# Gated delta rule with a ternary MLP: the value blocks are turned by VectorE and a trip through DRAM, not by TensorE

## The reference, cut to what matters

```python
# B=8 sequences, S=512 tokens, H=256; 16 key heads, 32 value heads (R=2 per key head), D=128, chunks of C=128
qkvz  = hidden @ W_qkvz                       # per key head: q, k, two v, two z
mixed = silu(causal_conv4(q | k | v))         # four taps along the sequence, per channel
beta, g = sigmoid(b), -exp(A_log) * softplus(a + dt_bias)
# per head, over chunks i:
T      = inverse(I + tril((beta*k) k^T * decay, -1))
v_new  = T (beta*v) ;  k_cum = T (beta*k*exp(g))
vn     = v_new_i - k_cum_i state
out_i  = (q_i*exp(g)) state + tril(q_i k_i^T * decay) vn
state  = state * exp(g_last) + (k_i*exp(g_last-g))^T vn
x = rmsnorm(out * silu(z)) @ W_out ; then layernorm, a gated MLP with ternary weights, layernorm
```

## Time and profile before

| | before |
|---|---|
| time, median of 3 runs | 4413.36 us (4413.11 to 4414.43) |
| the profiled execution: time | 4417.5 us |
| its span in the trace | 4415.7 us |
| mean granted TensorE clock | 0.989 of full speed |
| busy: PE, DVE, ACT, POOL | 4211.2 us (95%), 3725.5 us (84%), 3842.3 us (87%), 2334.8 us (53%) |
| DMA | 584.82 MB, mean 132 GB/s; 40.6% of 16 engines' time on SP's queue |

### The profile page before, as it was taken

How to read it: one execution, slowest core, us unless ns; L and a number is a source line. 1 busy time by engine, 2 the same in 40 slices (tenths; PEclk the granted TensorE clock), 3 DMA queues, 4 the chain that set the end, 5 groups by cost and what they waited for, 6 DMA issues and landing times. The chain is left out here.

```text
span 4415.7 us, 140088 instructions
## 1 busy us (share of the span) xinstructions
PE 4211.2 (95%) x44246; PEld 3699.2 (84%) x44246; DVE 3725.5 (84%) x6642; ACT 3842.3 (87%) x10855; POOL 2334.8 (53%) x3319
## 2 busy tenths in 40 slices
PE   3799999999999999999999999999999999999788
PEld 2688888888888888888888888888888888888645
DVE  5688888888888888888888888888888888888656
ACT  2699999999999999999999999999999999999655
POOL 3355555555555555555555555555555555555444
PEclk9899999999999999999999999999999999999989
DMA  5544444444444443434343434343434444444200
GB/s 183 179 134 143 134 140 134 140 135 140 137 138 142 132 147 128 151 125 153 123 154 121 154 120 154 120 154 121 153 124 150 129 145 133 141 134 141 70 10 29
DMA packets 450786, 584.82 MB, mean 132 GB/s; under 512 B 237472, under 2 KB 315552, under 8 KB 433184
## 3 DMA queue, kind: packets, MB, share of 16 engines
q1 hardware_dynamic: 449568, 575.59, 40.6%
q10 hardware_dynamic: 1152, 8.39, 0.5%
HBM read 533.81 MB, written 50.07 MB: 132 GB/s over the span
## 5 line engine op out<-in xcount | busy, mean ns | idle before, releaser
L1014 DVE SCALAR_TENSOR_TENSOR conv<-ps,cws,conv 128x511 f32<-128x511 f32 (+2 forms) x1536 | 1084.8, 741 | 59.3 <-ACT conv L892 39.3
L698 PE MATMUL ps<-xb,wb 128*128 128x512 f32 x3072 | 841.8, 409 | 26.0 <-DMA wb<-w_scratch 21.7
L698 PEld LDWEIGHTS ps<-xb,wb 128*128 128x128 f32 x3072 | 541.2, 189 | 129.2 <-issue 30.2
L1057 DVE CAST_PREDICATED pl<-masks,ps 128x512 f16<-128x512 uint16 x768 | 546.8, 712 | 55.3 <-PE ps L760 32.6
L953 ACT ACTIVATE t<-ps 128x512 f16<-128x512 f32 x768 | 465.8, 607 | 118.4 <-PE ps L768 107.3
L1263 POOL TENSOR_TENSOR xo<-xo,zs 128x512 f32<-128x512 f32 x128 | 164.0, 1281 | 714.3 <-DVE xo L1108 714.3
L1263 POOL TENSOR_TENSOR xo<-xo,home 128x512 f32<-128x512 f32 x128 | 163.0, 1273 | 699.8 <-DVE xo L1108 699.8
L957 ACT ACTIVATE u<-ps 128x512 f16<-128x512 f32 x768 | 473.1, 616 | 43.6 <-PE ps L773 43.6
L858 PE MATMUL ps<-wo,xt 128*128 128x256 f32 x3072 | 429.4, 289 | 33.4 <-DVE xt L1114 32.6
L712 PE MATMUL ps<-wb,xb 128*128 128x256 f32 x3072 | 428.3, 289 | 0.0
L858 PEld LDWEIGHTS ps<-wo,xt 128*128 128x128 f32 x3072 | 384.6, 191 | 47.4 <-issue 41.9
(11 more groups left out here) (188 smaller groups left out, 11691.8 us busy)
## 6 DMA issues: line engine op xcount, KB each, us to landing
xb<-x_scratch SPq DMA_DIRECT2D x128, 1024.0 KB, 5.8
wb<-w_scratch SPq DMA_DIRECT2D x128, 1024.0 KB, 5.7
decays<-rows_scratch SPq DMA_DIRECT2D x128, 512.0 KB, 3.7
wb<-w_scratch SPq DMA_DIRECT2D x128, 512.0 KB, 4.3
wo<-wout_scratch SPq DMA_DIRECT2D x128, 512.0 KB, 6.3
rk<-rk_scratch SPq DMA_DIRECT2D x128, 256.0 KB, 4.1
w_scratch<-wsplit SPq DMA_DIRECT2D x128, 192.0 KB, 3.2
wpiece<-in_Wqkvz SPq DMA_DIRECT2D x128, 96.0 KB, 2.5
```

The costliest lines, as they stand in the source:

```text
L698: last = nc.tensor.matmul(proj_bank[c][:, :], wb[:, pw, k * WCOL + c * D:k * WCOL + (c + 1) * D], xb[p][:, px, k * S:(k + 1) * S], start=( ...
L1014: nc.vector.scalar_tensor_tensor(out=conv[c][:, back:S], in0=proj_bank[c][:, 0:S - back], scalar=cws[p][:, c * TAPS + 3 - back:c * TAPS + ...
L1057: nc.vector.copy_predicated(halves(pl[l], l, 0), mask[:, None, :, :].broadcast_to([128, NU, C // (4 << l), 2 << l]), packed(p_bank, l)).th ...
```

## The change

PE no longer turns V0 and V1, and ACT no longer copies them. In their place:

- `flip` (twice, DVE): a transpose of `conv[V0 + h]` in blocks of 32 by 32, 128x512 float32 each time. Inside each group of 32 partitions a block is turned; blocks do not change their group. The output goes to `flip`, which lies in the memory of `et`.
- `move_v` (SP): when both flips are done, four stores, one for each 32-channel part `q`, each of 128 partitions by 1 KB, to `v_dram`, whose rows are ordered so that the DRAM side of each store runs over 4 outer rows, 32 rows inside, and 1 KB each. SP then waits until all four have landed, and loads the whole 512 KB into `vt[p]` with 4 KB for each partition.
- `vt[p]` has a new order, so `residual` reads runs of 32 elements. `residual 0` waits for the load (`vt_in`). `decay` waits for it as well, because `flip` lies in `et`; `flip` waits until `attn` has read `et`.
- `move_v` stands in the list right behind `flip 1`, ahead of `store_split` and `load_raw`.
- In the last iteration the load of the MLP's down weights (`ff_load 0`) moves from the end of one pass to a place behind `move_v` in the next, and waits for `vt_in`.
- Waits of PE, ACT and DVE that guarded the PSUM banks of the two turns go away.

```diff
+    v_dram = nc.dram_tensor("v_scratch", (4, 32, 4, R * NC * 32), f32, kind="Internal").ap()
...
-        vt = [home[:, 1, :].rearrange("p (n h d) -> p n h d", n=NC, h=R), sb("vt1", [128, NC, R, D])]
+        vt = [home[:, 1, :].rearrange("p (w x) -> p w x", w=4), sb("vt1", [128, 4, R * NC * 32])]
...
+        flip = et[:, :, :].rearrange("p (q u) c -> p q (u c)", q=4)
...
+        def values(p):
+            return vt[p][:, :, :].rearrange("p w (h n c) -> p n h w c", h=R, n=NC)
...
-            + at(-1, ("qs_mm", 1)) + at(0, ("turn", V0)) + at(-1, ("residual", 1), ("ff_tern", 0), ("ff_total", 2)) + at(1, ("tap", Q))
-            + at(-1, ("y", 1)) + at(0, ("t_copy", 0), ("small", 0), ("ff_load", 1), ("vt", 0), ("u_mm", 0)) + at(1, ("conv", Q, 1))
...
-               ("u_mm", 1), ("turn", V1), ("low", g0), ("p", 2)) + at(-1, ("ks_mm", 2)) + at(1, ("silu", K)) + at(-1, ("out", 1))
-            + at(0, ("u_copy", 1), ("t_mm", 2), ("vt", 1), ("ff_load", 2)) + at(1, ("split", 0), ("store_split", 0)) + at(2, ("load_raw", 0))
+            + at(-1, ("qs_mm", 1), ("residual", 1), ("ff_tern", 0), ("ff_total", 2)) + at(1, ("tap", Q)) + at(-1, ("y", 1)) + at(0, ("t_copy", 0),
+               ("small", 0), ("ff_load", 1), ("flip", 0), ("u_mm", 0)) + at(1, ("conv", Q, 1)) + at(-1, ("y_copy", 1)) + at(0, ("p_mm", 1))
...
+            + at(-1, ("ks_mm", 2)) + at(1, ("silu", K)) + at(-1, ("out", 1)) + at(0, ("u_copy", 1), ("t_mm", 2), ("flip", 1), ("move_v", 0),
+               ("ff_load", 2), ("ff_load", 0)) + at(1, ("split", 0), ("store_split", 0)) + at(2, ("load_raw", 0)) + at(0, ("u_mm", 2))
...
+            def move_v(a, p, _):
+                sp.wait_ge(flipped.sem, flipped.at(a, 2))
+                res_ready.wait(sp, a - 2, NC)
+                vt_in.wait(sp, a - 1, 16)
+                for q in range(4):
+                    sp.dma_start(v_dram[q].rearrange("r w x -> w r x"), flip[:, q, :]).then_inc(v_out.sem, 16)
+                sp.wait_ge(v_out.sem, v_out.at(a, 64))
+                sp.dma_start(vt[p][:, :, :], v_dram.rearrange("q r w x -> (q r) w x")).then_inc(vt_in.sem, 16)
...
                 if q == 0:
                     sys_ready.wait(sp, a, 2)
                     attn_ready.wait(sp, a, 2)
+                    vt_in.wait(sp, a, 16)
...
-                if c == V0:
-                    xt_low.wait(pe, a - 2, 2) or attn_ready.wait(pe, a, 2)
-                if c == V1:
-                    tapped.wait(pe, a + 1, convolved(K)) or z_ready.wait(pe, a, 1)
...
-            def values(a, p, h):
-                act.wait_ge(turn_mm.sem, turn_mm.at(a, h + 3))
-                res_ready.wait(act, a - 2, NC)
-                nc.scalar.activation(vt[p][:, :, h, :], four(turn_bank[V0 + h]), ACT.Copy).then_inc(vt_ready.sem, 1)
-
             def decay(a, p, g):
...
+                vt_in.wait(act, a - 1, 16)
...
+            def flip_v(a, p, h):
+                ve.wait_ge(silued.sem, silued.at(a, h + 3))
+                attn_ready.wait(ve, a, 2)
+                nc.vector.transpose(flip.rearrange("p q (h n c) -> p h q n c", h=R, n=NC)[:, h],
+                                    conv[V0 + h][:, :].rearrange("p (n q c) -> p q n c", n=NC, q=4)).then_inc(flipped.sem, 1)
...
-                    ve.wait_ge(vt_ready.sem, vt_ready.at(b, 2))
+                    ve.wait_ge(vt_in.sem, vt_in.at(b, 16))
...
-                                                          scalar=small[p][:, n, 0, h:h + 1], in1=vt[p][:, n, h, :],
+                                                          scalar=small[p][:, n, 0, h:h + 1], in1=values(p)[:, n, h],
```

More of the change, by code:

```diff
@@ L451, in delta_rule @@
         ff_bank = t_bank
[L452 removed]
+        turn_bank = (ps[7], ps[5], None, None)
         gram_bank = (ps[6], ps[7])
@@ L562, in delta_rule @@
[L562 to L579, removed]
@@ new lines, in delta_rule @@
+            + at(-1, ("qs_mm", 2)) + at(0, ("kw", 0), ("t_copy", 2), ("u_copy", 2)) + at(-1, ("residual", 2), ("ff_below", 1), ("ff_halves", 2),
+               ("y", 2)) + at(0, ("p_mm", 3)) + at(-1, ("gate", g0)) + at(1, ("conv", Q, 3)) + at(-1, ("o_square", g0), ("o_rnorm", g0))
+            + at(-2, ("added", g1)) + at(1, ("project", V0)) + at(0, ("p", 3)) + at(-1, ("y_copy", 2)) + at(0, ("t_mm", 3)) + at(1, ("turn", K))
+            + at(-1, ("q_part", 2)) + at(0, ("t_copy", 3)) + at(-1, ("update_mm", 2)) + at(0, ("u_mm", 3)) + at(-1, ("o_norm", g0), ("state", 2))
@@ new lines, in delta_rule @@
+            + at(0, ("low", g1), ("u_copy", 4), ("p_mm", 5)) + at(-1, ("y", 3), ("out", 2)) + at(0, ("p", 5)) + at(-1, ("qs_mm", 3))
+            + at(0, ("t_mm", 5)) + at(-1, ("y_copy", 3), ("x_low", g0)) + at(0, ("u_mm", 5)) + at(1, ("silu", Q), ("conv", V0, 2))
+            + at(-1, ("q_part", 3)) + at(1, ("conv", V1, 2), ("conv", V0, 3)) + at(-1, ("out_mm", g0)) + at(1, ("conv", V1, 3))
+            + at(0, ("u_copy", 5)) + at(1, ("mask_row", g1), ("keys", 0)) + at(0, ("t_copy", 5), ("ff_abs", 0), ("ff_abs", 1))
@@ new lines, in delta_rule @@
+            + at(-1, ("intra_mm", 3)) + at(0, ("resid_mm", g0)) + at(1, ("turn", Q)) + at(-1, ("added", g0), ("out", 3), ("ff_below", 2),
+               ("ff_tern", 2)) + at(0, ("ff_set", 0), ("resid_mm", g1)) + at(1, ("gram", g0)) + at(-1, ("gate", g1)) + at(1, ("gram", g1))
+            + at(0, ("resid", g0)) + at(1, ("decay", g0), ("squares", Q), ("decay", g1)) + at(2, ("load_rows", 0)) + at(1, ("system", g0))
+            + at(0, ("resid", g1), ("fix_mm", g0)) + at(1, ("attn", g0)) + at(0, ("residual", 0)) + at(1, ("project_z", g0)) + at(0, ("fix_mm", g1),
+               ("ff_total", 0), ("fix", g0)) + at(1, ("project_z", g1)) + at(2, ("load_wz", 0)) + at(3, ("load_x", 0)) + at(0, ("fix", g1),
+               ("ff_halves", 0), ("ff_below", 0)) + at(1, ("diagonal", g0)) + at(-1, ("o_square", g1)) + at(1, ("system", g1))
@@ L671, in ff_load @@
                 else:
-                    turn_mm.wait(sp, a, 4)
+                    flipped.wait(sp, a, 2)
+                    silued.wait(sp, a, 4)
+                    kq_ready.wait(sp, a, 1)
                 src = (io["WdownT"], io["WupT"], io["WgateT"])[q]
@@ L675, in ff_load @@
                 sp.dma_start(FF_RAW[q].rearrange("p (k n) -> p k n", k=k), src.rearrange("(k p) n -> p k n", p=128)).then_inc(ff_in[q].sem, 16)
-            steps(sp, ff_load=ff_load, load_w=load_w, load_wz=load_wz, load_x=load_x, load_raw=load_raw, store_split=store_split, load_rows=load_rows, store_norm=store_norm, load_norm=load_norm, load_wout=load_wout)
+            steps(sp, ff_load=ff_load, load_w=load_w, load_wz=load_wz, load_x=load_x, load_raw=load_raw, store_split=store_split, load_rows=load_rows, store_norm=store_norm, load_norm=load_norm, move_v=move_v, load_wout=load_wout)
         @block.tensor
@@ L693, in project @@
                 if c == V0:
-                    vt_ready.wait(pe, a - 1, 2) or tapped.wait(pe, a, convolved(K))
+                    tapped.wait(pe, a, convolved(K))
                 if c == V1:
@@ L1179, in ff_ternary @@
                     link(nc.vector.tensor_tensor(m["fs"][:, 1:2], fscale[:, 0:1], fsud[:, :], ALU.mult))
-            steps(ve, ff_set=ff_set, ff_halves=ff_halves, ff_below=ff_below, ff_tern=ff_ternary, conv=convolve, keys=keys, system=system, attn=attention, u_first=first, t_first_copy=t_first_copy, p=factor,
+            steps(ve, ff_set=ff_set, ff_halves=ff_halves, ff_below=ff_below, ff_tern=ff_ternary, conv=convolve, flip=flip_v, keys=keys, system=system, attn=attention, u_first=first, t_first_copy=t_first_copy, p=factor,
                   resid=resid, fix=fix, residual=residual, state=state, out=output, x_low=x_low, added=add)
```

34 lines of the change are left out of this document (20 added, 14 removed).

## The result

The changed kernel takes 5329.56 us by the median of 4 runs (5325.63 to 5339.91), the kernel before 4413.23 us beside it. The ratio is 1.208, with a 95% interval of 1.206 to 1.2101: a fifth slower. The forecast was 5360 us with a range of 4800 to 5750; the measured time lies inside it. The profiled execution has a span of 5338.3 us, 922.6 more than before.

What follows compares the result with a forecast made beforehand. PE set the pace before; afterwards a ring through SP's queue would bind: 20.0 + 2.0 + 16.8 = 38.8 us a pass, 7.4 more. 4417.5 + 127 x 7.38 + 5 = 5360 us, range 4800 to 5750.

Steps and rivals of the forecast that it cites:

- the ring through SP's queue: From `keys` through `flip 1`, SP's stores and loads, norm's store and load back to `keys`: 36.8 us without the clock's cost.
- the four engines: Stores with four outer DRAM rows run on four DMA engines at 102.5 GB/s: 5.1 us for 512 KB.
- the clock: PE's idle time before `gram` drops the granted clock to 0.50, adding 2.0 us a pass.
- `keys` to the end of `flip 1`, clock included: DVE's stretch: 19.07 us plus 1.4 of flips less 0.5 hidden, 20.0, plus 2.0 for the falling clock.
- end of `flip 1` to the values' load: SP issues the four stores and waits until they land: 0.41 + 1.42 + 5.1 = 6.9 us.
- load and four issues: On SP, the load's issue, 0.41 us, and four dynamic-address issues of 0.84 each: norm's store follows 3.8 us behind.
- norm's store to its load: SP's norm store behind the values' load and four smaller transfers: 2.0 us, between 1.42 alone and 4.85 with a full queue.
- norm's load to `keys`: The norm's load lands 4.1 us after its issue, by the median, and `keys` waits for it.
- The case with a clock that holds: Four engines, but PE's clock does not fall: 36.8 us a pass, 5106 us; chance 0.08.
- The rival of sixteen engines: Stores use all DMA engines, term 3.4 us: pass 33.3 us, 4661 us, or 4915 with falling clock; chance 0.14.
- The rival of the flips alone: Flips delay `p`, which PE waits for, by half a microsecond; queue doesn't bind: pass 31.9 us, 4480 us; chance 0.02.
- The faster rival: Queue hides the stores, DVE's waits swallow the flips, PE stays the bound and saves 116 us: 4302 us; chance 0.04.

Runs made afterwards that it cites:

- the kernel with the steady clock: Against the changed kernel, 45 extra transposes of the identity fill PE's wait before `gram`, clock steady at 1.00: 5091.4 us.
- the first experiments: Against the changed kernel, the stores' DRAM side got 128 outer rows, values at wrong partitions: 4487.4 us; or 32 outer rows, values at their own partitions: 4541.7 us.
- the best order without transfers: Against the kernel with flips but no values' transfers, both flips behind `residual 2`, activation sum and third Q convolution behind `p 3`: 4376.6 us.

## Why the prediction was right, step by step

The mechanism was the one that the prediction named: the ring through SP's queue, the four engines and the clock. The sum is closer than its terms are. Predicted and measured, from the rows of SP and DVE above and as the mean of the trace's 127 passes:

| term, us a pass | predicted | measured in this pass | mean |
|---|---|---|---|
| `keys` to the end of `flip 1`, clock included | 20.0 + 2.0 | 2048.83 - 2026.99 = 21.84 | 21.19 |
| end of `flip 1` to the values' load | 6.9 | 2056.93 - 2048.83 = 8.10 | 8.14 |
| load and four issues | 3.8 | 2060.61 - 2056.93 = 3.68 | 3.78 |
| norm's store to its load | 2.0 | 2062.28 - 2060.61 = 1.67 | 1.91 |
| norm's load to `keys` | 4.1 | 2066.08 - 2062.28 = 3.80 | 3.62 |
| sum | 38.8 | 39.09 | 38.63 |

By the means the stores' term was 1.2 us too short, the stretch from `keys` to `flip 1` 0.8 too long and the norm's load 0.5 too long. That these errors cancel to 0.2 us is luck; that each term is within 1.3 us of its measure is not.

- *From `keys` to `flip 1`.* The prediction let 0.9 of the flips' 1.4 us show in this stretch. In the kernel with the steady clock it takes 19.07 us by the mean, just what the prediction read from `keys` to `out 1` alone, so next to nothing of the flips shows there (whether the removed turns gave it back was not tried apart); the clock accounts for the other 2.1 of 21.19.
- *Four engines.* Shown by the first experiments and the packets in flight. The term was 1.2 us short. The four issues took 2.34 us, 0.58 each, where the earlier trace rows have 0.41, and four engines moved 86 GB/s together instead of the quarter of 410 GB/s, 102.5; 512 KB at 86 GB/s are 6.1 us instead of 5.1.
- *The clock.* 2.0 us was taken from the second pass; the filled wait gives 1.94. The case with a clock that holds was put at 36.8 us and 5106; the kernel in which it holds has 36.69 and 5091, with the same errors cancelling.
- *The flips.* 0.70 us, from `conv`'s row; 256 of them took 0.703 by the median. The Trainium skill's 311 ns for 128x128 bf16 ("VectorE: DVE Perf Modes", The three transpose paths) gave an estimate of 1.24 us for 512 columns; the trace has 0.703 us in float32, so the measurement decides against that estimate.
- *What would show it.* PE's gap before `gram` came to 5.56 us in the row above; 5 to 7 were named. The last of the four stores landed 7.89 us after the first issue by the median (5 or more were named). The norm's store went out 11.8 us behind `flip 1` (10 or more were named), and the clock was at 0.50 behind `gram`.
- *The last pass.* 5 us were added; 922.6 - 916 leaves 7 for the start and the last pass together, which no run takes apart.
- *The rival of sixteen engines* was put at 33.3 us and 4661. The kernel with 32 outer rows has 32.36 and 4542: from the end of `flip 1` to the load it took 3.9 us by the median (3.4 were expected), but the stretch from `keys` to `flip 1` took 19.1 us instead of 20.0 and the norm's load 3.6 instead of 4.1, and the clock held.
- *The rival of the flips alone* was put at 4480, and measured at 4437. It was put down to PE's wait for `p`; that wait grew by 34 us, from 94.0 to 127.8, but the wait for `residual`, which was not named, grew by 113, from 0.7 to 113.6.
- *The faster rival*, 4302, did not appear even where nothing was moved. The 0.91 us a pass that the removed turns held on PE, 116 us, is the term that the runs do not bear out: in the best order without transfers 41 us of the span came through, 4415.7 to 4375.0. PE's busy time fell by 63 us (4211.2 to 4147.8), and PE's waits for ACT's `u` grew from 1.8 to 34.5 us. Why the busy time fell by 63 and not by 116 is left open.
- *The residuals*, for whose new reading order nothing was taken, cost nothing more: 339 and 336 ns an instruction in the changed kernel's two buffers, 345 and 344 before.

## What to carry to other kernels

Here a pass was as long as its longest ring of waits, and a queue that waited for a landing made everything behind it in the list part of that ring; look at what stands behind the wait, and what of it another engine needs. Count the outer rows of a transfer before its bytes: the same 512 KB took 5.5 us or 1.9 us of SP's wait, by how they were cut. Look, too, at what stands behind new work on the engine that receives it: here one step's place in DVE's order, without the values' transfers, decided between 0.4% slower and 0.8% faster.

## What had not been expected of the hardware

- A backlog on four DMA engines slows the issues behind it as well: one small load's issue took 1.41 us instead of 0.47, and the norm's store of 2 KB 3.23 us to the next issue instead of 1.42. With one store of 128 rows in that place the medians are 0.44 and 1.43.
- A 2 KB store issued 0.48 us behind a load of 512 KB took 3.18 us to the next issue; issued 3.68 us behind it, with four small transfers between them, it took 1.67. Whether the time or the transfers between them matter was not tried.
- The four engines moved 86 GB/s at a DMA share of 0.27; with 32 outer rows, and pieces of the same 1 KB, it was 178 GB/s at 0.71. Estimated from the share, that is 16 x 0.27 = 4.3 busy engines with 20 GB/s each, and 11.4 with 15.7 each.
